# GpSimd's list scatters in a two-layer sandwich kernel: six at a step's end split in three and three, and the last eight spread in pairs over four blocks

## The chip, the cores and the metric

The kernel runs on one core of a Trainium2 chip. The metric is device time in microseconds of one execution. A core has five engines with an instruction queue each: TensorE (PE in the profile), VectorE (DVE), ScalarE (ACT), GpSimd (POOL) and SyncE (SP), which here only issues DMAs. Each executes its own queue in order; they meet through semaphores.

## The reference, cut to what matters

The input is 4096 tokens of 128 numbers (16 sequences of 256). A layer of causal linear attention with 16 heads is followed by a mixture of experts (a shared one and 8 routed ones, 2 for each token), each with a LayerNorm before and after.

```python
x = x + layernorm(attention(layernorm(x)))
xf = layernorm(x)
shared = gelu(xf @ Wfc_s + bfc_s) @ Wproj_s + bproj_s
probs = softmax(xf @ Wr)                       # 8 experts
topk_p, topk_i = top_k(probs, 2)               # gates, renormalised
routed = sum over e of (gelu(xf @ Wfc[e] + bfc[e]) @ Wproj[e] + bproj[e]) * gate[:, e]
x = x + layernorm(shared + routed)
```

## The kernel before

**Two phases.** The first goes through the tokens in NS = 8 groups of 512 (a group is 4 tiles of 128 tokens). The function `iteration(i, head, tail, nxt, routed)` of each engine is one step: in step i the head does group i's attention, the tail group i-1's output norms, and the routed part sends group i-2's tokens to their experts. Steps 0, 1, 2, 7 and 8 are written out; steps 3 to 6 are one hardware loop (`all_iterations`, L338 to L348). The second phase goes through NB = 39 blocks of 256 rows, each of one expert: `step(b, n, turn)` of each engine does block b's part of a pipeline three blocks deep.

**Lists.** Each expert has a list of rows in device memory (`expert_lists`). For each group, ScalarE copies the normed rows twice, with the number of the result row behind each (`rows_of`), VectorE works out a place in the lists for each (`route_pos`), and GpSimd writes them with eight indirect DMAs, one for each tile and choice (`scatters(i, first, last)`, L675, issued at L686). In step i the eight scatters are group i-2's.

**GpSimd's order in a step** (L741 to L791) is written by hand. In a step of the loop it is: `inv_std(1, i)` (L620 to L627, the norm of the attention's output, which waits for VectorE's `mean_var`, L1609); `route_gaps` and `route_chosen` (L694, L701); the last two scatters of the step before; `last_pairs` (L710, a fourth of the products of keys and values); Z parts 0, 1 and 2 (L767, L777, L782, factors of TensorE's output products at L1311), with the residual X (L772) and `placed` and `acc` (L733, L735) between them; `inv_std2` (L610 to L615, the norm before the experts); and then scatters 0 to 5 of this step. In step 7 scatters 0 to 4 stand there, and in step 8 the order is another.

**The logits' copy** is `a.activation(lg...)` at L1057 on ScalarE. It frees the bank in which TensorE then sums the denominators (L1414), and VectorE's `route_top` (L1705) starts from it. It increments `lg_read`, first in step 2, so that after step i's copy the semaphore stands at i-1. Ahead of it ScalarE has in a step: the rest of x (L1020), the switch of its table (L1021) and the next group's first norm (L871).

**Blocks.** In block b GpSimd's `scatter_block` waits for `blk_yr`, which VectorE raises once block b's results are in SBUF (L2124), and issues two indirect DMAs into `expert_results` (L807). At its b = 2 it first issues all eight scatters of the last group (NS - 1), whose places VectorE has ready in its own step 4. SyncE loads each block's weights (L468, 578 KB) and rows (L475, 129 KB), up to NBUF = 6 blocks ahead. Blocks 0 to 12 are made from rows of the groups scattered early; ahead of block 13 (CLOSES_AT) SyncE waits in `lists_closed` (L449 to L453) for all scatters of all groups (`scattered_late`, L452) and for the lists' tails. TensorE turns block b's rows at L1355 and multiplies at L1505 to L1507 and L1532.

Of the kernel before, what the change touches and what calls it, by code (L numbers as in the profile page):

```python
# [19 lines left out]
TILES = 4  # L20
# [21 lines left out]
def sandwich_kernel(nc, x, w_qkv, b_qkv, w_out, b_out, wfc_s, bfc_s, wproj_s, bproj_s, wr, wfc, bfc, wproj,  # L42
# [4 lines left out]
    NS = TOKENS // STEP  # L47
# [31 lines left out]
    with ExitStack() as ctx:  # L79
# [6 lines left out]
        def sem(name):  # L86
            return ctx.enter_context(nc.semaphore(name))
# [211 lines left out]
        s = {n: sem(n) for n in names}  # L299
# [9 lines left out]
        def alone(eng):  # L309

            eng.sem_inc(s["waited"], 1)
# [54 lines left out]
        def second_set(i):  # L366

            return int(isinstance(i, int) and i == NS)
# [167 lines left out]
        def _(pool):  # L536
# [36 lines left out]
            def inv_std0_early():  # L573

                a, b = TILES, 4 * TILES
                pool.wait_ge(s["ln0_mv"], 4)
                g.tensor_scalar(ve0[:, a:b], mv0[:, a:b, 1], 1.0, LN_EPS, ALU.mult, ALU.add)
                g.tensor_scalar(neg_mean0[:, a:b], mv0[:, a:b, 0], -1.0, None, ALU.mult)
                g.tensor_scalar(neg_sum0[:, 0:b], mv0[:, 0:b, 0], -float(D), None, ALU.mult
                                ).then_inc(s["ve0_ready"], 1)  # L580
                pool.wait_ge(s["ve0_ready"], 2)
                root0(a, b, 2)
# [34 lines left out]
            def inv_std(which, count):  # L617

                pool.wait_ge(s[f"ln{which}_mv"], count)
                g.tensor_tensor(ve[:, which], mv[:, which, :, 1], ln_eps[:], ALU.add)  # L620
                g.tensor_tensor(neg_mean[:, which], mv[:, which, :, 0], minus_one[:], ALU.mult
                                ).then_inc(s[f"ve{which}_ready"], 1)
                pool.wait_ge(s[f"ve{which}_ready"], count)
                g.tensor_tensor(rstd[:, which], ve[:, which], neg_half[:, 0:TILES], ALU.pow
                                ).then_inc(s[f"pow{which}_done"], 1)
                pool.wait_ge(s[f"pow{which}_done"], count)
                g.tensor_tensor(shift[:, which], neg_mean[:, which], rstd[:, which], ALU.mult  # L627
                                ).then_inc(s[f"ln{which}_rstd"], 1)
# [46 lines left out]
            def scatters(i, first, last):  # L675

                if first == 0:
                    pool.wait_ge(s["pos_ready"], i - 1)
                    pool.wait_ge(s["rows_ready"], i - 1)
                    alone(pool)  # L680
                pos, rows = pos_of_step[second_set(i)], rows_of_step[second_set(i)]
                landed = s["scattered"]
                if isinstance(i, int) and i - 2 >= COUNTED:
                    landed = s["scattered_mid" if i - 2 == COUNTED else "scattered_late"]
                for m in range(first, last):
                    g.indirect_dma_start(  # L686
                        out=lists, out_offset=bass.IndirectOffsetOnAxis(ap=pos[:, m:m + 1], axis=0),
                        in_=rows[:, m // TILES, m % TILES, :], in_offset=None).then_inc(landed, 16)

            def route_gaps(i):  # L690

                pool.wait_ge(s["top_ready"], 2 * TILES * (i - 2) + TILES)
                gaps = gap[:, bass.ds(TILES * (i - 2), TILES)]
                g.tensor_tensor(gaps, top[:, :, 1], top[:, :, 0], ALU.subtract).then_inc(s["idx_ready"], 1)  # L694

            def route_chosen(i):

                pool.wait_ge(s["hot_ready"], i - 1)
                if from_on(i, 3):
                    pool.wait_ge(s["rank_done"], i - 2)  # L700
                g.tensor_tensor(chosen[:], onehot[:, 0], onehot[:, 1], ALU.add).then_inc(s["chosen_ready"], 1)  # L701

            def last_pairs(i):

                pool.wait_ge(s["k_copied"], i + 3)
                if from_on(i, 1):
                    pool.wait_ge(s["z_ready"], 3 * i)
                for pair in range(3 if from_on(i, FREE) else 2, 4):
                    pool.wait_ge(vr_in[pair], 64 * (i + 1))
                    g.tensor_tensor(KV[:, 2 * pair:2 * pair + 2], keys.unsqueeze(1).broadcast_to([P, 2, STEP]),  # L710
                                    vr[:, 2 * pair:2 * pair + 2], ALU.mult).then_inc(s["kv_last"], 1)
# [10 lines left out]
            def rest_of_weights():  # L722

                pool.wait_ge(s["w1s_hi"], 1)
                g.tensor_tensor(w1s_lo[:], w1s_sb[:], w1s_hi[:].bitcast(F32), ALU.subtract
                                ).then_inc(s["w1s_lo"], 1)
# [10 lines left out]
            def before_next(i):  # L737

                return 5 if isinstance(i, int) and i == NS - 1 else 6

            def iteration(i, head, tail, nxt, routed):  # L741

                if isinstance(i, int) and i == 1:
                    last_pairs(1)
                if tail:
                    inv_std(1, i)
                if isinstance(i, int) and i == 0:
                    inv_std0_early()
                if isinstance(i, int) and i == 1:
                    rest_of_weights()  # L750
                if head and routed:
                    route_gaps(i)
                    route_chosen(i)
                if from_on(i, 3) and head:
                    scatters(i - 1, before_next(i - 1), 2 * TILES)
                if isinstance(i, int) and i == 0:
                    means_late()
                if head and not (isinstance(i, int) and i == 1):
                    last_pairs(i)
                if not head:  # L760
                    scatters(i - 1, before_next(i - 1), 2 * TILES)
                if head:
                    pool.wait_ge(s["kv_sum"], 4 * i + 1)
                    pool.wait_ge(s["qn_copied"], i + 1)
                    if from_on(i, 1):
                        pool.wait_ge(s["out_done"], i)
                    g.tensor_tensor(Z[:, 0], KV[:, 0], qn[:], ALU.mult).then_inc(s["z0_ready"], 1)  # L767
                if tail:
                    pool.wait_ge(s["attn_ready"], i)
                    sum_of_x1(i)  # L770
                    Xs = X[:, bass.ds(TILES * (i - 1), TILES), :]
                    g.tensor_tensor(Xs, Xs, attn[:], ALU.add).then_inc(s["x1_ready"], 1)  # L772
                if not head:
                    scatters(i, 0, 1)
                    inv_std2(i)
                if head:
                    g.tensor_tensor(Z[:, 1], KV[:, 1], qn[:], ALU.mult).then_inc(s["z1_ready"], 1)  # L777
                if head and routed:
                    route_placed(i)
                if head:  # L780
                    pool.wait_ge(s["kv_sum"], 4 * i + 2)
                    g.tensor_tensor(Z[:, 2], KV[:, 2], qn[:], ALU.mult).then_inc(s["z1_ready"], 1)  # L782
                if isinstance(i, int) and i == 0:
                    zeds_of_first()
                if tail and head:
                    inv_std2(i)
                if isinstance(i, int) and i == 1:
                    inv_std0_late()
                    fill_pads()
                if routed:  # L790
                    scatters(i, 0 if head else 1, before_next(i) if head else 2 * TILES)  # L791

            all_iterations(pool, iteration)

            def scatter_block(b, n, turn):
                if isinstance(b, int) and b == 2:
                    scatters(NS + 1, 0, 2 * TILES)
                last = isinstance(b, int) and b >= NB - HALVED
                if last:
                    pool.wait_ge(s["half_yr"], b + 1 - NB + HALVED)  # L800
                else:
                    pool.wait_ge(s["blk_yr"], b + 1)
                    alone(pool)
                for c in range(2):
                    if last and c:
                        pool.wait_ge(s["blk_yr"], b + 1)
                    g.indirect_dma_start(  # L807
                        out=results,
                        out_offset=bass.IndirectOffsetOnAxis(ap=yrow[n][:, c], axis=0),
                        in_=yb[n][:, c, :], in_offset=None).then_inc(blk_scat[n], 16)  # L810
# [1397 lines left out]
```

## Time and profile before

| | |
|---|---|
| median of 3 executions | 372.18 us |
| lowest, highest | 369.17 us, 475.82 us |
| the profiled execution: its span | 373.1 us |
| TensorE busy in it | 336.1 us (90%) |
| GpSimd busy in it | 275.8 us (74%) |
| mean granted clock of TensorE | 0.979 of full speed |

The span is from the first to the last instruction of one profiled execution, the only figure that the profile has for its own time. "Busy" is the time in which an engine had an instruction in execution; an indirect DMA counts on GpSimd for as long as GpSimd takes to write its descriptors, and the data move after that. The busy shares are averages over both phases.

### The profile page before, as it was taken

The numbers are of one execution on the slowest core, as the hardware profiler recorded it, in microseconds if no ns is written. First come the engines' busy times: TensorE is split into PE (matmuls) and PEld (weight loads), VectorE is DVE, ScalarE is ACT, GpSimd is POOL, SyncE is SP. The second block draws the span as 40 slices with busy tenths as digits, with TensorE's granted clock in tenths as the row PEclk, the third lists the DMA queues.
The fourth block names the chain that finished last, engine by engine and source line by source line (L and its number), as shares of the span: only waits on it lengthen the run. The fifth ranks groups of instructions, "written<-read, shape, count | busy, mean of one in ns | idle before, by whom it ended". The sixth has DMA issues, their size and how long they took to land.

```text
span 373.1 us, 8565 instructions
## 1 busy us (share of the span) xinstructions
PE 336.1 (90%) x2515; PEld 293.8 (79%) x2522; DVE 286.7 (77%) x716; ACT 271.3 (73%) x700; POOL 275.8 (74%) x365
## 2 busy tenths in 40 slices
PE   7767878998889889989989989979999999999993
PEld 3437457787678768877868879979999999999973
DVE  4999886999889888988995666764545539888766
ACT  4959467889868877888855878644665576689774
POOL 7878787877977869678788887777775556588760
PEclk9989999999999998989999999998999999999998
DMA  6576743967282520712605926997988769999237
GB/s 203 157 214 185 177 138 89 186 175 187 85 220 68 147 92 14 199 47 67 174 23 159 321 77 195 275 269 254 279 259 258 253 217 362 375 295 285 71 128 226
DMA packets 53515, 69.09 MB, mean 185 GB/s; under 512 B 6365, under 2 KB 37386, under 8 KB 53482
## 3 DMA queue, kind: packets, MB, share of 16 engines
q1 hardware_dynamic: 47556, 58.58, 54.7%
q0 software_dynamic: 4544, 9.35, 7.4%
q10 hardware_dynamic: 1382, 0.79, 0.8%
q8 instruction: 12, 0.20, 0.2%
q14 instruction: 21, 0.17, 0.1%
HBM read 40.06 MB, written 18.15 MB: 156 GB/s over the span
## 4 chain that ended last, share of the span: by engine, by line
PE 32%; POOL 16%; issue 11%; DVE 7%; DMA 6%; ACT 6%; SPq 2%; ACTq 1%; POOLq 1%; DVEq 0%
PE bO L1532 6%; PE bO L1311 5%; PE bS L1532 5%; DMA xb<-expert_lists 5%; POOL expert_results L807 4%; POOL expert_lists L686 2%; POOL KV L710 2%; POOL Z L777 2%; POOL X L772 2%; PE bA L1283 2%; PE bV L1506 1%; PE bV L1507 1%; PE bV L1505 1%; DMA expert_results<-yb,yrow 1%; POOL Z L767 1%
## 5 line engine op out<-in xcount | busy, mean ns | idle before, releaser
L807 POOL DMA_INDIRECT expert_results<-yb,yrow x78 | 79.2, 1015 | 36.7 <-issue 20.2
L686 POOL DMA_INDIRECT expert_lists<-rows,pos x64 | 65.0, 1016 | 22.4 <-issue 21.8
L1683 DVE TENSOR_TENSOR_SCAN KV<-bS,KV 128x1024 f32<-128x1024 bf16 x32 | 72.8, 2277 | 0.8
L1311 PE MATMUL bO<-wout_rot,Z 128*128 128x128 f32 x512 | 63.5, 278 | 7.7 <-POOL Z L777 2.3
L1311 PEld LDWEIGHTS bO<-wout_rot,Z 128*128 128x128 f32 x512 | 60.1, 192 | 12.5 <-POOL Z L777 3.2
L1137 ACT ACTIVATE hs<-bV,KV 128x256 f32<-128x256 f32 x56 | 21.9, 474 | 13.0 <-PE bV L1507 13.0
L1532 PE MATMUL bO<-KV,hs 128*128 128x128 f32 x232 | 30.1, 284 | 0.8 <-ACT hs L1137 0.8
L2116 DVE COPY yrow<-xb 128x2 int32<-128x2 int32 x24 | 4.6, 193 | 33.2 <-PE bO L1532 16.7
L1283 PE MATMUL bA<-w2s_sb,hs 128*128 128x128 f32 x224 | 30.1, 285 | 0.0
L1532 PEld LDWEIGHTS bO<-KV,hs 128*128 128x128 f32 x232 | 28.5, 199 | 1.3 <-ACT hs L1137 1.3
L1283 PEld LDWEIGHTS bA<-w2s_sb,hs 128*128 128x128 f32 x224 | 28.0, 200 | 0.1
L710 POOL TENSOR_TENSOR KV<-shared,vr 128x1024 f32<-128x1024 f32 x10 | 23.6, 2361 | 5.9 <-ACT shared L963 5.6
L1674 DVE TENSOR_TENSOR KV<-bV,vr 128x1024 f32<-128x1024 f32 x22 | 25.8, 1200 | 0.0
L1505 PE MATMUL bV<-x_lo,w_hi 128*128 128x256 f32 x80 | 24.0, 300 | 0.0
L1532 PE MATMUL bS<-Z,hs 128*128 128x128 f32 x192 | 23.3, 275 | 0.0
L1532 PEld LDWEIGHTS bS<-Z,hs 128*128 128x128 f32 x192 | 22.4, 192 | 0.0
L1506 PE MATMUL bV<-x_hi,w_hi 128*128 128x256 f32 x80 | 22.4, 280 | 0.0
L1507 PE MATMUL bV<-x_hi,w_lo 128*128 128x256 f32 x80 | 22.4, 279 | 0.0
L1691 DVE TENSOR_TENSOR Z<-KV,bV 128x1024 f32<-128x1024 f32 (+1 forms) x22 | 21.6, 1010 | 0.0
L1137 ACT ACTIVATE hs<-bA,Z 128x256 f32<-128x256 f32 x24 | 10.1, 470 | 14.9 <-PE bB L1507 14.9
L856 ACT ACTIVATE xn<-X,shift,rstd 128x128 f32<-128x128 f32 (+1 forms) x32 | 13.2, 483 | 8.6 <-POOL shift L615 8.3
L856 ACT ACTIVATE shared<-bO,shift,rstd 128x128 f32<-128x128 f32 x32 | 14.2, 462 | 4.4 <-POOL shift L627 4.4
(373 smaller groups left out, 1005.7 us busy)
## 6 DMA issues: line engine op xcount, KB each, us to landing
KV<-packed_weights SPq DMA_DIRECT2D x21, 578.0 KB, 5.1
Z<-packed_weights SPq DMA_DIRECT2D x18, 578.0 KB, 5.4
xb<-expert_lists SPq DMA_DIRECT2D x39, 129.0 KB
vr<-vr SPq DMA_DIRECT2D x16, 224.0 KB, 2.5
shared<-expert_results SPq DMA_DIRECT2D x7, 512.0 KB, 5.5
vr<-vr SPq DMA_DIRECT2D x16, 192.0 KB, 2.5
vr<-vr SPq DMA_DIRECT2D x16, 160.0 KB, 2.4
vr<-vr SPq DMA_DIRECT2D x16, 128.0 KB
```

The lines of the kernel that those rows point to most:

```text
L686: g.indirect_dma_start(out=lists, out_offset=bass.IndirectOffsetOnAxis(ap=pos[:, m:m + 1], axis=0), in_=rows[:, m // TILES, m % TILES, :], ...
L710: g.tensor_tensor(KV[:, 2 * pair:2 * pair + 2], keys.unsqueeze(1).broadcast_to([P, 2, STEP]), vr[:, 2 * pair:2 * pair + 2], ALU.mult).then ...
L807: g.indirect_dma_start(out=results, out_offset=bass.IndirectOffsetOnAxis(ap=yrow[n][:, c], axis=0), in_=yb[n][:, c, :], in_offset=None).th ...
L856: ins = a.activation(dst(j), src(j), ACT.Identity, bias=shift[:, which, j:j + 1], scale=rstd[:, which, j:j + 1], accum_out=None if total i ...
L1137: ins = a.activation(hb[m % 2][:, c], blk_h[m % 2][c // 2][:, (c % 2) * BLK:(c % 2 + 1) * BLK], ACT.Gelu_apprx_tanh, bias=wb[m][:, B1_AT + ...
L1283: ins = t.matmul(bA[:, j * D:(j + 1) * D], hs[:, c, j * P:(j + 1) * P], w2s_sb[:, c], start=False, stop=True, skip_group_check=True)
L1311: ins = t.matmul(bO[:, j * D:(j + 1) * D], Z[:, d, j * P:(j + 1) * P], wout_rot[:, d], start=False, stop=True, skip_group_check=True)
L1505: t.matmul(h, w[0], x_lo[m % 2][:], start=True, stop=False)
L1506: t.matmul(h, w[0], x_hi[m % 2][:], start=False, stop=False)
L1507: ins = t.matmul(h, w[1], x_hi[m % 2][:], start=False, stop=True)
L1532: ins = t.matmul(bank_y[:, r * D:(r + 1) * D], hb[m % 2][:, c, r * P:(r + 1) * P], wb[m][:, HID + c * D:HID + (c + 1) * D], start=(c == 0 ...
L1683: v.tensor_tensor_scan(w, ps_keep, w, 0.0, ALU.mult, ALU.add).then_inc(s["kv_sum"], 1)
```

## The change

In steps 2 to 6 GpSimd issues scatters 0, 1 and 2 at the step's end, then waits until `lg_read` is at least i, then issues scatters 3, 4 and 5. `alone` is an instruction that only increments a semaphore nobody waits for. Step 7 (five scatters at the end) and step 8 stay as they were. In the block phase `scatters(NS + 1, ...)` is called for blocks 2 to 5 with two scatters each, each pair ahead of that block's own two result scatters. Nothing else differs.

```diff
                 if isinstance(i, int) and i == 1:
                     inv_std0_late()
                     fill_pads()
-                if routed:
+                if routed and head and not (isinstance(i, int) and i == NS - 1):
+                    scatters(i, 0, 3)
+                    pool.wait_ge(s["lg_read"], i)
+                    alone(pool)
+                    scatters(i, 3, before_next(i))
+                elif routed:
                     scatters(i, 0 if head else 1, before_next(i) if head else 2 * TILES)
...
             def scatter_block(b, n, turn):
-                if isinstance(b, int) and b == 2:
-                    scatters(NS + 1, 0, 2 * TILES)
+                if 2 <= b < 2 + TILES:
+                    scatters(NS + 1, 2 * (b - 2), 2 * (b - 2) + 2)
                 last = isinstance(b, int) and b >= NB - HALVED
```

## Rows read from the trace of the kernel before

**Rows 1.** The page: the span, and each engine's busy time, share and instructions.

```profile
span 373.1 us, 8565 instructions
PE 336.1 (90%) x2515; PEld 293.8 (79%) x2522; DVE 286.7 (77%) x716; ACT 271.3 (73%) x700; POOL 275.8 (74%) x365
```

**Rows 2.** Timeline, GpSimd, one step: start, duration, line, tiles [idle before <-releaser].

```profile
127.66 0.20 POOL L615 TENSOR_TENSOR shift<-neg_mean,rstd 128x4 f32<-128x4 f32 x1
128.45 1.09 POOL L686 DMA_INDIRECT expert_lists<-rows,pos  x1 [0.58 <-issue]
129.84 1.24 POOL L686 DMA_INDIRECT expert_lists<-rows,pos  x1 [0.30 <-issue]
...
135.17 0.95 POOL L686 DMA_INDIRECT expert_lists<-rows,pos  x1 [0.30 <-issue]
137.61 0.20 POOL L620 TENSOR_TENSOR ve<-mv,ln_eps 128x4 f32<-128x4 f32 x1 [1.48 <-DVE mv L1609]
...
149.16 1.26 POOL L782 TENSOR_TENSOR Z<-KV,shared 128x512 f32<-128x512 f32 x1
151.45 0.19 POOL L610 TENSOR_SCALAR ve<-sq 128x4 f32<-128x4 f32 x1 [1.03 <-ACT shared L902]
```

**Rows 3.** Timeline, ScalarE, the logits' copy in the same step.

```profile
136.46 0.17 ACT L1057 ACTIVATE lg<-bB 128x32 f32<-128x32 f32 x1
```

**Rows 4.** Timeline, VectorE, the same step.

```profile
129.55 0.69 DVE L1936 SCALAR_TENSOR_TENSOR shared<-shared 128x512 f32<-128x512 f32 x1
...
137.16 0.36 DVE L1609 BATCH_NORM_AGGREGATE mv<-bst 128x2 f32<-128x6 f32 x4
...
149.12 0.22 DVE L1756 TENSOR_REDUCE pos<-placed 128x8 int32<-128x64 f32 x1 [0.16 <-POOL placed L733]
149.25 2.34 DVE L1691 TENSOR_TENSOR Z<-KV,bV 128x1024 f32<-128x1024 f32 x2
```

**Rows 5.** Chain of waits that ended last, the same step's end: start, length, what.

```profile
150.56 4.73 PE bO L1311 x40
...
160.49 0.86 ACT shared L871 x2
```

**Rows 6.** Timeline, ScalarE: the copy in step 3 and in step 7.

```profile
87.32 0.17 ACT L1057 ACTIVATE lg<-bB 128x32 f32<-128x32 f32 x1
184.61 0.17 ACT L1057 ACTIVATE lg<-bB 128x32 f32<-128x32 f32 x1
```

**Rows 7.** Timeline, GpSimd: the first instruction of `inv_std(1)` in step 3 and in step 7.

```profile
88.46 0.20 POOL L620 TENSOR_TENSOR ve<-mv,ln_eps 128x4 f32<-128x4 f32 x1 [0.42 <-DVE mv L1609]
186.91 0.20 POOL L620 TENSOR_TENSOR ve<-mv,ln_eps 128x4 f32<-128x4 f32 x1 [0.48 <-DVE mv L1609]
```

**Rows 8.** Timeline, GpSimd, block phase: last group's first and last scatter, then blocks'.

```profile
234.88 0.96 POOL L686 DMA_INDIRECT expert_lists<-rows,pos  x1 [0.31 <-issue]
...
244.51 0.96 POOL L686 DMA_INDIRECT expert_lists<-rows,pos  x1 [0.31 <-issue]
245.77 1.41 POOL L807 DMA_INDIRECT expert_results<-yb,yrow  x1 [0.30 <-issue]
...
254.31 0.95 POOL L807 DMA_INDIRECT expert_results<-yb,yrow  x1 [0.30 <-issue]
```

**Rows 9.** One line's instructions (L452): xcount: duration min/median/max, first and last start.

```profile
L452 SPq EVENT_SEMAPHORE  x1: 28/28/28, 252.5 to 252.5; - x1
```

**Rows 10.** Line L686 over the whole span: time from issue to landing.

```profile
DMA to landing us min/median/max: 2.3/5.2/8.1
```

**Rows 11.** Timeline, SyncE's queue: block 13's rows are issued.

```profile
255.82 0.38 SPq L475 DMA_DIRECT2D xb<-expert_lists  x1
```

**Rows 12.** Chain of waits, block phase: TensorE turns block 13's rows.

```profile
262.65 0.22 PE bH L1355 x2
```

**Rows 13.** Two steps: stretch, length, busy (x instructions) by engine, PEclk, DMA share, GB/s.

```profile
112.10:136.60 24.50, 21.59 (x154) 18.11 (x155) 21.74 (x39) 20.17 (x49) 19.73 (x26) 1.00 0.40 113
136.60:161.40 24.80, 22.98 (x154) 19.60 (x155) 21.92 (x39) 20.32 (x50) 19.17 (x26) 0.93 0.33 95
```

## The prediction, on record before the result

> **What bounds the kernel now.** I began with the page [rows 1]: TensorE is busy 90% of the 373.1 us and GpSimd 74%, but these are averages over two phases, and the first part of the change acts in the first phase alone. So I read one step of the loop, engine by engine, to see who waits for whom at the place that the change touches.
>
> GpSimd's timeline [rows 2] has six scatters from 128.45 to 136.12 (first, second and last are shown; the three between took 0.95 to 0.96 us, with 0.30 us ahead of each), then 1.48 us of idle time until VectorE's `mean_var` [rows 4] ended at 137.5, then `inv_std(1)` at 137.61. From there to 150.42, the end of Z part 2 (L782), GpSimd has no wait of any size: `inv_std(1)`, two scatters, L710, three Z parts, X, `placed`. Who needs their end? VectorE sat 0.16 us until GpSimd's `placed` before it could reduce the places, and its last two Z parts stand behind that [rows 4]. TensorE's forty output products start at 150.56, 0.14 us behind GpSimd's Z part 2, and the chain of waits goes through them and on to ScalarE's L871 ahead of the next logits' copy [rows 5]. So a step is a loop: copy, mean_var, GpSimd's run of 12.8 us, TensorE's products, the norm's transposes, ScalarE, next copy. The period is 24.5 to 24.8 us [rows 13]. What the reader is to see: the six scatters at the step's end are not on that loop. They fill time in which GpSimd would only wait for `mean_var`, and 1.48 us is left over.
>
> **First part of the change, the wait.** After step i's copy `lg_read` is i-1, so a wait for i in step i is a wait for the copy of step i+1. In the shown step it ended at 136.63 [rows 3]. Scatters 0 to 2 would be issued at about 132.3, after which GpSimd idles 4.3 us. It then has three scatters to do where it had none: the start after a release, at 0.6 us (the 0.58 us ahead of the first scatter at 128.45), then 1.05 + 0.30 + 0.96 + 0.30 + 0.96 = 3.57 us (the first of a run near 1.09, the later ones at 0.96, the gaps 0.30) [rows 2]. So `inv_std(1)` starts 4.25 us behind the copy (136.63 + 4.25 = 140.9) instead of 137.61, which is 0.98 us behind it. The step's loop is 3.27 us longer.
>
> Queued behind the waiting instruction are three scatters and then the whole run that TensorE and VectorE wait for. What could absorb it? `mean_var` needs only the copy and stays. ScalarE's norm of the attention output would start late, but is not last at Z part 0. VectorE's sum of the last pair waits for L710 and starts late with it, VectorE's 0.16 us wait for `placed` becomes 3.4 us, TensorE's wait for Z the same. The 1.03 us that GpSimd idles for ScalarE's squares [rows 2] lies behind Z part 2, beside the forty products, and I read it as slack of the second norm alone: it gives nothing back to the loop. I cost no gain from it.
>
> The wait stands at the end of steps 2 to 6, so it meets the copies of steps 3 to 7, five times. In step 3 the distance from copy to `inv_std(1)` is 88.46 - 87.49 = 0.97 us, and I take the same for steps 4 and 6. In step 7 it is 186.91 - 184.78 = 2.13 us, because the early table's work stands ahead of `mean_var` on VectorE there [rows 6, 7]. There the delay is 4.25 - 2.13 = 2.1 us. Sum: 4 x 3.27 + 2.1 = **15.2 us**.
>
> Bounds of this term: with a start of 0.15 us and the shortest scatters throughout (3 x 0.96 + 2 x 0.30 = 3.48) it is 3.63 us behind the copy, 2.65 a step, 12.1 in all. Above, if each moved scatter were stretched as the second one in [rows 2] is (1.24 against 0.96), 0.84 us more a step, 19.4 in all.
>
> That second scatter is worth a look. It ran beside VectorE's L1936 at 129.55 [rows 4], whose operands all lie in SBUF; the others ran beside instructions with an operand in PSUM. I take 0.96 us for the moved ones, since what follows the copy on VectorE (maxima, statistics, the product of keys and values from PSUM) is no such instruction. The Trainium skill, "SBUF — State Buffer", section "Who interferes with whom", says that VectorE and GpSimd share one pair of SBUF ports under an exclusive lock, taken by VectorE when it has two SBUF inputs or runs in its two-port mode. By that rule the step's end is a bad place for descriptor writing and a place behind the copy a good one, which speaks for the change; what it would give back is the 0.28 us of one scatter, which stays where it is. With it or without it the sum is 15.2.
>
> The moved scatters' data land 8 us later than now. `rows_of` and `route_pos` of the next step wait for all eight of a group, of which the last two are issued behind `inv_std(1)` as before, so these set that wait and move with the step. No cost of its own.
>
> **Second part, the pairs.** GpSimd now issues the last group's eight scatters from 234.88 to 245.47 and then the results of block 2 and on, running late on all of them [rows 8]. With pairs, the results of blocks 2, 3 and 4 (six scatters) come ahead of the eighth. Six took from 245.77 to 254.31, 8.5 us, so the eighth starts at 253.0 instead of 244.5 on the clock of now. The number of instructions is the same and GpSimd is back in step with VectorE at the same time; the results of blocks 2 to 4 land sooner, for which nobody was waiting.
>
> Who waits for the eighth is SyncE, ahead of block 13: its wait for it passed at 252.5, 8.0 us after the issue [rows 9]. Landing takes 2.3 to 8.1 us, median 5.2 [rows 10]. The new wait ends at 255.3 to 261.1, at 258.2 with the median: 5.7 us later (2.8 to 8.6). Block 13's rows were issued at 255.82 [rows 11] and turned by TensorE at 262.65 [rows 12], 6.8 us of room. Issued 5.7 us later, at 261.5, they land between 2.3 us on (the shortest landing of a smaller transfer) and 6.8 us on (they were there in that time now). I take 3.7 us, nearer the short end, since the queues run empty while SyncE waits: 265.2, and TensorE stalls **2.5 us**. The early end with the short landing gives no stall, the late one with 6.8 us gives 8.6. The loads of block 14 and on come late too, but TensorE is then late as well, so it costs once.
>
> **Sum.** 373.1 + 15.2 + 2.5 = 390.8 on the profiled span. That span lies 0.9 above the median of the runs, and the lowest run 3.0 below the median; the same sum on the median gives 389.9. I say 389.
>
> **Rivals.**
>
> TensorE's clock adds to it. In the second of the two steps [rows 13] the granted clock was 0.93 in the mean: (1 - 0.93) x 24.8 / 0.5 = 3.5 us of it at the lower level, 1.2 of 2.4 GHz. That step was 0.3 us longer. With 3.3 us more of idle time in each step there may be more such stretches. If each of five took 1.7 us of the forty products (3.5 us at half speed), that is 8.5 more: 398. Against it: a step with the same idle time ran at 1.00.
>
> Part of the delay is absorbed. If VectorE's and TensorE's paths beside GpSimd's have less need of it than I read (for instance GpSimd's two later scatters overlap with a wait that I can't see), the step grows by 1.5 instead of 3.3 and the block phase by nothing: 372.2 + 7.5 = 380. For it: the 1.03 us of idle time ahead of `inv_std2`. Against it: 0.16 and 0.14 us are all the slack the rows show.
>
> Not slower: the copy is done before GpSimd asks for it. Its place is the wait at the end of the step, its price zero, and it decides where the copy comes before 132.3, the end of scatter 2; then the three scatters follow without a gap and all stays at 372. It needs the release to be 4.3 us earlier than the copy in [rows 3], or the semaphore to run one step ahead of my count. A gain over 2% would need scatters that hold up VectorE or ScalarE now; the rule on the shared port is what could give that, and VectorE's idle times there are for the copy and not for GpSimd.
>
> **How the numbers follow.** 0.74 for the forecast (384 to 394), 0.12 for the clock (394 to 399), 0.08 for the part absorbed (378 to 384), 0.06 for no delay. A change of 2%, 7.4 us, is about what a measurement of this kernel can tell from none: below 379.6 is "same". The last case is nearly all same, with 0.01 of it for a gain, and the absorbed case gives 0.01 to it as well. The range takes the forecast with the lower end of the first term (372.2 + 12.1 = 384, and 2 less for a low median) up to most of the clock's case: 382 to 398.
>
> **What would show it.** Right: GpSimd idle 4 us ahead of the fourth scatter with ScalarE's copy as its end; no more idle time ahead of L620; the copies in steps 4 to 6 some 27.8 us apart instead of 24.6; VectorE 3 us idle ahead of L1756; SyncE's L452 passed some 5.7 us later on the block phase's own clock, and TensorE idle for block 13's rows. Wrong: copies still 24.6 us apart (the delay was hidden), or more than 28.5 apart with a clock well under 0.9 (the clock took its share), or a block phase of unchanged length (the second part is free).

## The result and the profile after

The changed kernel took 392.1 us in the median of 4 runs (389.21 to 394.11), the kernel before 373.0 us in the median of 4. The ratio is 1.0541, with a 95% interval of 1.0493 to 1.0589: 20 us slower. Runs more than 1.5% above the fastest of the same kernel, such as the one of 475.82 us of the kernel before, stand in the medians of this document and not in its ratios. The profiled execution has a span of 387.5 us against 373.1, only 14.4 more, because the two profiled executions are not typical ones: that of after was the fastest of its four runs (389.21 us, 1.7 above its span), while that of before, whose span alone is 373.1, lies above its kernel's median.

```profile
span 387.5 us, 8570 instructions
PE 341.8 (88%) x2515; PEld 295.4 (76%) x2522; DVE 285.5 (74%) x716; ACT 272.0 (70%) x700; POOL 275.0 (71%) x365
```

Beside [rows 1], VectorE, ScalarE and GpSimd are busy for the same time to within 1.2 us, in a longer span; GpSimd's is even 0.8 less. What was added is waiting, and 5.7 us of TensorE, which is busy longer with the same number of instructions. The timeline of GpSimd over a step's end, after (start, duration, line, tiles, idle time before and its releaser), is the counterpart of [rows 2]:

```profile
134.67 1.09 POOL L686 DMA_INDIRECT expert_lists<-rows,pos  x1 [0.58 <-issue]
136.06 1.25 POOL L686 DMA_INDIRECT expert_lists<-rows,pos  x1 [0.30 <-issue]
137.62 0.96 POOL L686 DMA_INDIRECT expert_lists<-rows,pos  x1 [0.30 <-issue]
144.36 0.96 POOL L686 DMA_INDIRECT expert_lists<-rows,pos  x1 [5.78 <-ACT lg L1062]
145.62 0.96 POOL L686 DMA_INDIRECT expert_lists<-rows,pos  x1 [0.30 <-issue]
146.88 0.96 POOL L686 DMA_INDIRECT expert_lists<-rows,pos  x1 [0.30 <-issue]
147.86 0.22 POOL L620 TENSOR_TENSOR ve<-mv,ln_eps 128x4 f32<-128x4 f32 x1
```

(Lines behind 790 stand 5 further on in the changed kernel: the copy is L1062 there, `mean_var` L1614.) The copy ended at 143.54. The fourth scatter starts 0.82 us behind it, and L620, the head of the run that everybody waits for, 4.32 us behind it. In [rows 2, 3] that distance was 0.98. The 1.48 us for which GpSimd waited for `mean_var` are gone from the row of L620.

Now the whole time, stretch by stretch. The cuts are the logits' copy of steps 3 to 7, TensorE's turning of block 0, of block 9 and of block 14, and the end. Each row of this view has: from and to, length, busy time of PE, PEld, DVE, ACT and POOL with instruction counts, TensorE's granted clock, DMA share, GB/s. First the kernel before:

```profile
87.32:111.92 24.60, 21.60 (x154) 18.11 (x155) 21.73 (x39) 20.21 (x50) 20.46 (x27) 1.00 0.58 151
111.92:136.46 24.54, 21.59 (x154) 18.11 (x155) 21.74 (x39) 20.21 (x49) 19.73 (x26) 1.00 0.40 114
136.46:161.26 24.80, 22.98 (x154) 19.60 (x155) 21.92 (x39) 20.32 (x49) 19.03 (x26) 0.93 0.33 95
161.26:184.61 23.35, 22.47 (x157) 19.41 (x159) 20.84 (x35) 18.86 (x46) 18.34 (x26) 0.93 0.34 98
184.61:210.02 25.41, 23.27 (x168) 19.25 (x167) 18.97 (x74) 15.66 (x42) 21.62 (x31) 1.00 0.42 137
210.02:244.77 34.75, 32.72 (x301) 31.80 (x300) 23.82 (x87) 26.97 (x69) 27.36 (x30) 1.00 0.72 202
244.77:265.90 21.13, 19.07 (x152) 18.74 (x151) 10.37 (x31) 10.21 (x26) 16.30 (x16) 0.92 0.92 263
265.90:373.10 107.20, 100.50 (x854) 97.89 (x852) 72.41 (x243) 74.54 (x193) 64.73 (x67) 0.99 0.77 250
```

The same eight stretches of the kernel after:

```profile
85.02:114.80 29.78, 24.69 (x154) 20.81 (x155) 21.83 (x39) 20.46 (x49) 19.74 (x26) 0.89 0.51 135
114.80:143.37 28.57, 24.37 (x154) 20.53 (x155) 21.94 (x39) 20.54 (x49) 19.73 (x26) 0.88 0.28 83
143.37:171.24 27.87, 22.48 (x154) 18.32 (x155) 21.83 (x39) 20.48 (x49) 19.71 (x26) 1.00 0.29 85
171.24:197.73 26.49, 21.96 (x157) 18.41 (x159) 21.41 (x38) 18.99 (x46) 19.72 (x26) 1.00 0.30 89
197.73:226.44 28.71, 24.86 (x168) 19.82 (x167) 18.65 (x72) 15.46 (x42) 23.64 (x33) 0.94 0.39 118
226.44:260.17 33.73, 32.51 (x302) 31.75 (x301) 22.77 (x87) 26.86 (x69) 26.05 (x29) 1.00 0.72 214
260.17:280.80 20.63, 17.72 (x152) 17.15 (x151) 10.53 (x31) 10.31 (x26) 16.05 (x16) 1.00 0.85 246
280.80:387.50 106.70, 100.60 (x854) 97.83 (x852) 72.40 (x243) 74.44 (x193) 64.31 (x68) 0.99 0.80 255
```

The differences are +5.18, +4.03, +3.07, +3.14, +3.30, then -1.02, -0.50 and -0.50. They make +16.7, and the copy of step 3 came 2.3 us earlier, a difference that stands already at step 2's copy, where the two kernels are alike: +14.4. So the loss lies in the five steps, as +18.7 us, and the block phase of this execution lost nothing against this execution of before.

The cleanest pair is 27.87 against 24.54, both at a clock of 1.00: **+3.33 us a step.** The first two steps lost more, at a granted clock of 0.89 and 0.88. TensorE's forty products show it, in its timeline after:

```profile
98.13 1.16 PE L1316 MATMUL bO<-wout_rot,Z 128*128 128x128 f32 x8 [1.81 <-POOL Z L767]
100.72 2.08 PE L1316 MATMUL bO<-wout_rot,Z 128*128 128x128 f32 x8 [1.43 <-POOL Z L777]
103.01 6.07 PE L1316 MATMUL bO<-wout_rot,Z 128*128 128x128 f32 x40 [0.22 <-issue]
```

They took 6.07 us here and 4.73 in [rows 5]. TensorE had sat idle 1.8 and 1.4 us for GpSimd's Z just ahead; then the eight products and the first half of the forty ran at the lower level (the granted clock of 100 to 106 is 0.50). The same idle times stand in steps 5 and 6, which ran at 1.00, so the idle time does not decide it. Over steps 3 to 6 of the profiles taken where the kernel before takes 371 to 373 us, 13 of 16 steps were below 1.00 in the four profiles of kernels with scatters behind the copy (9 of 12 without the long run of four and two), and 6 of 20 in the five profiles of kernels with none. More idle time and more such steps go together here; that one makes the other is not shown. The kernel before is one of the latter: its two steps at 0.93 had the lower level just behind the logits' copy (0.50 from 163 to 166 in the second), after TensorE had sat idle for 1.2 us.

VectorE, after, waited for GpSimd in two places instead of the one of [rows 4]:

```profile
155.19 2.29 DVE L1688 TENSOR_TENSOR_SCAN KV<-bS,KV 128x1024 f32<-128x1024 bf16 x1 [3.14 <-POOL KV L710]
...
159.36 0.22 DVE L1761 TENSOR_REDUCE pos<-placed 128x8 int32<-128x64 f32 x1 [1.30 <-POOL placed L733]
```

In the block phase, TensorE's turning of blocks 10, 12 and 13 after:

```profile
264.06 0.44 PE L1360 MATMUL bT<-ident,xb 128*128 128x128 f32 x2 [0.37 <-DMA xb<-expert_lists]
...
271.58 0.38 PE L1360 MATMUL bT<-ident,xb 128*128 128x128 f32 x2
277.33 0.44 PE L1360 MATMUL bH<-ident,xb 128*128 128x128 f32 x2 [2.16 <-DMA xb<-expert_lists]
```

Block 13 stalled for its rows, 5.75 us behind block 12 where 3.42 is the undisturbed distance. SyncE's side of it, after: its wait for the scatters, and the issue of block 13's rows, beside [rows 9, 11].

```profile
L452 SPq EVENT_SEMAPHORE  x1: 28/28/28, 271.4 to 271.4; - x1
```

```profile
273.41 0.38 SPq L475 DMA_DIRECT2D xb<-expert_lists  x1
```

But before had a stall of its own, at block 10, in its TensorE timeline:

```profile
244.77 0.38 PE L1355 MATMUL bH<-ident,xb 128*128 128x128 f32 x2
...
250.41 0.44 PE L1355 MATMUL bT<-ident,xb 128*128 128x128 f32 x2 [2.06 <-DMA xb<-expert_lists]
...
255.65 0.38 PE L1355 MATMUL bH<-ident,xb 128*128 128x128 f32 x2
```

From block 9 to block 14 it took 21.13 us where five undisturbed blocks take 17.1: 4.0 lost, with a stretch of low clock behind the stall (block 10 to 11 took 5.24). That is why the table shows no loss there. The four other kernels that issue the last eight in a row (the split alone, four and two, seven and eight at the end, below) stalled for 0.5 to 1.5 us at block 10 and took 18.5 to 19.5 us for that stretch, so this profile of before is the long one of its kind.

### The profile page after: what moved, and what is told of

The parts are those of the page before. It is cut to its first block, busy times and chain, and to the rows that moved or that the text cites. A ratio compares the mean times of both kernels' runs of the same rounds, so it can differ in the third digit from the quotient of the medians.

```text
span 387.5 us, 8570 instructions
## 1 busy us (share of the span) xinstructions
PE 341.8 (88%) x2515; PEld 295.4 (76%) x2522; DVE 285.5 (74%) x716; ACT 272.0 (70%) x700; POOL 275.0 (71%) x365
## 4 chain that ended last, share of the span: by engine, by line
PE 37%; POOL 19%; issue 12%; ACT 8%; DMA 3%; DVE 3%; POOLq 1%; ACTq 1%; SPq 0%; DVEq 0%
PE bO L1316 9%; PE bO L1537 6%; PE bS L1537 6%; POOL expert_lists L686 4%; POOL expert_results L812 4%; POOL KV L710 3%; ACT shared L861 2%; POOL Z L767 2%; PE bV L1511 2%; POOL Z L777 2%; PE bV L1510 2%; PE bV L1512 2%; POOL X L772 2%; ACT shared L876 1%; DMA xb<-expert_lists 1%
## 5 line engine op out<-in xcount | busy, mean ns | idle before, releaser
L812 POOL DMA_INDIRECT expert_results<-yb,yrow x78 | 78.0, 1000 | 36.1 <-issue 19.3
L686 POOL DMA_INDIRECT expert_lists<-rows,pos x64 | 65.8, 1028 | 46.1 <-ACT lg L1062 25.6
L1316 PE MATMUL bO<-wout_rot,Z 128*128 128x128 f32 x512 | 67.8, 289 | 20.6 <-POOL Z L767 10.3
L1316 PEld LDWEIGHTS bO<-wout_rot,Z 128*128 128x128 f32 x512 | 63.8, 202 | 27.7 <-POOL Z L767 14.3
L1537 PE MATMUL bO<-KV,hs 128*128 128x128 f32 x232 | 28.9, 277 | 0.8 <-ACT hs L1142 0.8
L1288 PE MATMUL bA<-w2s_sb,hs 128*128 128x128 f32 x224 | 29.0, 278 | 0.0
L1537 PEld LDWEIGHTS bO<-KV,hs 128*128 128x128 f32 x232 | 27.2, 192 | 1.3 <-ACT hs L1142 1.3
L1288 PEld LDWEIGHTS bA<-w2s_sb,hs 128*128 128x128 f32 x224 | 26.8, 193 | 0.1
L710 POOL TENSOR_TENSOR KV<-shared,vr 128x1024 f32<-128x1024 f32 x10 | 23.5, 2355 | 4.3 <-ACT shared L968 3.8
L1202 PE MATMUL bH<-zeros 128*128 128x512 bf16 x56 | 17.6, 471 | 1.6 <-POOL bias_raw L539 1.3
```

Source lines behind the costliest of these rows:

```text
L686: g.indirect_dma_start(out=lists, out_offset=bass.IndirectOffsetOnAxis(ap=pos[:, m:m + 1], axis=0), in_=rows[:, m // TILES, m % TILES, :], ...
L812: g.indirect_dma_start(out=results, out_offset=bass.IndirectOffsetOnAxis(ap=yrow[n][:, c], axis=0), in_=yb[n][:, c, :], in_offset=None).th ...
L1288: ins = t.matmul(bA[:, j * D:(j + 1) * D], hs[:, c, j * P:(j + 1) * P], w2s_sb[:, c], start=False, stop=True, skip_group_check=True)
L1316: ins = t.matmul(bO[:, j * D:(j + 1) * D], Z[:, d, j * P:(j + 1) * P], wout_rot[:, d], start=False, stop=True, skip_group_check=True)
L1537: ins = t.matmul(bank_y[:, r * D:(r + 1) * D], hb[m % 2][:, c, r * P:(r + 1) * P], wb[m][:, HID + c * D:HID + (c + 1) * D], start=(c == 0 ...
```

## Experiments

**Theories.** Mine: in each of five steps the scatters behind the copy delay the head of GpSimd's run, the loop grows by what they take, and the pairs add a stall at block 13. Rivals: the wait itself (a release, an instruction more) is what costs; TensorE's clock is the larger part; the pairs carry the loss.

The first runs of the split alone, the pairs alone, the wait behind six and four and two met a chip on which the kernel before takes 413 us, and the second run of the wait behind six one on which it takes 420. All others met a chip on which it takes 371 to 372. Only the latter carry sizes.

### The split alone (two runs)

```diff
-                if routed:
+                if routed and head and not (isinstance(i, int) and i == NS - 1):
+                    scatters(i, 0, 3)
+                    pool.wait_ge(s["lg_read"], i)
+                    alone(pool)
+                    scatters(i, 3, before_next(i))
+                elif routed:
```

> The wait and the three scatters behind it in steps 2 to 6, with the last group's eight scatters as before. Theory (the three scatters stand on GpSimd's run, which the step's loop goes through; the pairs cost 2.5 us at block 13 on their own): steps some 3.3 us longer where the clock stays up, the first phase 15 to 19 us longer, ratio 1.042 to 1.052; no stall ahead of block 13's rows. Rival (the pairs give back about what they cost, as the block phase of the changed kernel, no longer than before, suggests): the same ratio as the whole change, 1.054 within 0.004.

Measured: 418.68 us, ratio 1.0234 (1.0138 to 1.0330), against 413.42.

> The split alone again, now that the kernel before takes 372 us in other calls. Theory: nearly the whole cost, ratio 1.042 to 1.055, copies of steps 3 to 6 27.7 to 29.8 us apart. If the pairs carry 2.5 us on their own, this is 0.007 under the whole change; if they give back what they cost, it is the same within 0.004.

Measured: 391.19 us, ratio 1.0539 (1.0481 to 1.0597), against 371.2. The split alone is the whole loss as far as these two ratios can tell: 0.007 for the pairs would be within their intervals. Its timeline shows the same picture as after (L620 at 118.41, its step's copy ended at 114.07: 4.34 us behind). On the slower chip the steps of an unsplit kernel are longer already. There the profile of the pairs alone, whose steps are those of the kernel before, shows the copy late (ScalarE idles 0.8 to 1.7 us ahead of it with no releaser in the core's own record) and more idle time ahead of L620 than the 1.48 us of [rows 2]:

```profile
142.00 0.20 POOL L620 TENSOR_TENSOR ve<-mv,ln_eps 128x4 f32<-128x4 f32 x1 [2.66 <-DVE mv L1609]
```

Its copies are 26.7 to 27.1 us apart in steps 3 to 6, those of the split kernel there 28.0 to 29.6. So the same edit costs some 2 us a step there.

### The pairs alone (two runs)

```diff
-                if isinstance(b, int) and b == 2:
-                    scatters(NS + 1, 0, 2 * TILES)
+                if 2 <= b < 2 + TILES:
+                    scatters(NS + 1, 2 * (b - 2), 2 * (b - 2) + 2)
```

> The last group's eight scatters in pairs over blocks 2 to 5, the steps' ends as before. Theory (they cost a stall for block 13's rows and give nothing): 2.5 us, ratio 1.004 to 1.010, SyncE passes L452 some 5 to 8 us later, TensorE idle 2 us ahead of block 13's rows. Rival (they also ease the load of block 10's rows, for which TensorE stalled 2.06 us before): that stall goes and the sum is near zero, ratio 0.997 to 1.003.

Measured: 414.45 us, ratio 1.0081 (1.0023 to 1.0138). This profile has no stall at block 13 (3.42 us behind block 12), so on the slower chip the cause of these 0.8% stays open.

> The pairs alone again. Theory of the prediction (a stall of 2.5 us for block 13's rows, nothing back): ratio 1.004 to 1.010. Rival (block 10's rows, for which TensorE stalled 2.06 us before, come sooner, since half of the descriptors ahead of them go elsewhere or the phase differs): 0.997 to 1.003, with a stall at block 13 and none at block 10. Last time it was 1.008 on a chip on which the kernel before took 413 us.

Measured: 375.72 us, ratio 1.0123 (1.0075 to 1.0171): 4.6 us of 371.2 (2.8 to 6.3). The pairs do cost, and more than I had said. The rival was right that block 10 does not stall here, and wrong that this makes up for block 13. The turning of blocks 12, 13 and 14 in TensorE's timeline of this kernel:

```profile
254.81 0.38 PE L1355 MATMUL bT<-ident,xb 128*128 128x128 f32 x2
261.56 0.69 PE L1355 MATMUL bH<-ident,xb 128*128 128x128 f32 x2 [3.02 <-DMA xb<-expert_lists]
266.35 0.38 PE L1355 MATMUL bT<-ident,xb 128*128 128x128 f32 x2
```

The stall is 3.02 us, block 13 comes 6.75 us behind block 12 and block 14 another 4.79 behind it, both beyond 3.42, at a lowered clock: 4.7 us in all. The wait for the scatters ended here at

```profile
L452 SPq EVENT_SEMAPHORE  x1: 28/28/28, 255.4 to 255.4; - x1
```

that is 45.7 us behind block 0 (turned at 209.66), where it is 42.5 before.

### The last eight as four and four

```diff
-                if isinstance(b, int) and b == 2:
-                    scatters(NS + 1, 0, 2 * TILES)
+                if 2 <= b < 4:
+                    scatters(NS + 1, 4 * (b - 2), 4 * (b - 2) + 4)
```

> The last group's eight scatters as four and four, ahead of the results of blocks 2 and 3; the steps' ends as before. Only block 2's two results come ahead of the eighth, so it goes 2.5 us later instead of 8.5. Theory (block 13's rows are late by what the eighth is late, less the slack, which was near none for 5.7 us): SyncE passes L452 about 2 to 3 us later than before, no stall or one under 0.5 us at block 13, ratio 0.996 to 1.003. Rival (any order but eight first costs the pairs' amount): 1.004 or more.

Measured: 372.6 us, ratio 1.0025 (0.9983 to 1.0068). With two results between the scatters instead of six, no loss can be told: the eighth scatter starts at 245.23, not at 252.14 as with pairs, SyncE passes at 251.5 (43.7 us behind block 0, 1.2 later than before, where I had expected 2 to 3), and TensorE's stretch from block 9 to block 14 lost 1.0 us. The windows' row of that stretch, first of the kernel with the pairs alone:

```profile
244.36:266.35 21.99, 18.97 (x152) 18.46 (x151) 10.45 (x31) 10.32 (x26) 16.81 (x18) 0.92 0.83 248
```

And of the kernel with fours:

```profile
242.50:260.57 18.07, 17.70 (x153) 17.14 (x151) 10.37 (x31) 10.30 (x26) 13.79 (x15) 1.00 0.91 268
```

The two differ by 3.9 us, the two medians by 3.1.

### The wait kept, all six scatters ahead of it (two runs)

```diff
-                if routed:
+                if routed and head and not (isinstance(i, int) and i == NS - 1):
+                    scatters(i, 0, 6)
+                    pool.wait_ge(s["lg_read"], i)
+                    alone(pool)
+                    scatters(i, 6, before_next(i))
+                elif routed:
```

(`before_next(i)` is 6 there, so nothing is behind the wait.)

> All six scatters at the step's end, and the wait for the logits' copy behind them with nothing moved behind it. Theory (the cost is the three scatters behind the wait, not the wait): GpSimd waits there for the copy and then for mean_var as before, L620 some 1 us behind the copy, ratio 0.997 to 1.004. Rival (the wait itself, its release and the instruction behind it, costs): 0.5 us or more a step, 2.5 us or more, ratio over 1.007.

Measured: 412.44 us, ratio 1.0030 (0.9979 to 1.0080).

> The whole six scatters of a step ahead of the wait for the logits' copy, nothing behind it, on a chip on which the kernel before takes about 372 us. Theory: the harm of the split is the scatters that are left behind the copy (1.26 us each and 0.8 us of release), not the wait. With none behind it, the wait ends before GpSimd's next line 620 could start anyway (0.98 us behind the copy in the kernel before, 0.8 us of it being release), so the ratio is 0.995 to 1.008 and line 620 starts within 0.5 us of where it does before. Rival: the wait in itself holds GpSimd (a slow release in each of five steps, at 0.8 us each): ratio 1.01 or more, line 620 at 1.8 us behind the copy.

Measured: 416.39 us, ratio 0.9999 (0.9949 to 1.0049). Both runs met slower chips, where L620 has more slack, so the claim holds for these. There the wait costs nothing. Its timeline, GpSimd, last scatter and L620; the copy of that step ended at 120.11:

```profile
117.10 0.96 POOL L686 DMA_INDIRECT expert_lists<-rows,pos  x1 [0.30 <-issue]
121.08 0.20 POOL L620 TENSOR_TENSOR ve<-mv,ln_eps 128x4 f32<-128x4 f32 x1 [3.02 <-DVE mv L1614]
```

L620 starts 0.97 us behind the copy, as in the kernel before in [rows 2, 3] (0.98), although GpSimd waited for the copy first: `mean_var` and its release end later than that wait. The rival that the wait itself holds GpSimd would have put it later. Of the 0.98 us nothing is the release of such a wait, as the expectation had it: L620 starts 0.09 us behind the end of `mean_var` in [rows 2, 4].

### Four ahead of the copy and two behind (two runs)

The edit is that of the split alone with 4 for 3 in both calls.

```diff
+                    scatters(i, 0, 4)
+                    pool.wait_ge(s["lg_read"], i)
+                    alone(pool)
+                    scatters(i, 4, before_next(i))
```

> Four scatters ahead of the wait and two behind it, the eight as before. Theory (each scatter behind the wait lengthens the step by its 1.26 us): L620 3.0 us behind the copy instead of 4.25, steps 2.0 us longer, 8 to 11 us in all, ratio 1.022 to 1.031. Rival (what counts is that GpSimd is held until the copy at all): the same as three and three, ratio 1.042 or more.

Measured: 418.46 us, ratio 1.0207 (1.0085 to 1.0330).

> Four ahead of the wait, two behind it. Theory (1.26 us a step for each scatter behind the wait): L620 3.0 us behind the copy, 4 x 2.0 + 0.9 = 8.9 us, ratio 1.020 to 1.030. Rival (holding GpSimd until the copy is what costs): 1.042 or more.

Measured: 386.11 us, ratio 1.0306 (1.0237 to 1.0375), between none behind and three behind. The ratio rests on the runs of 381.28 and 383.94 us alone, and the profile is of one of the two longer ones (388.27). GpSimd's timeline; the copy of this step ended at 145.62:

```profile
146.43 0.96 POOL L686 DMA_INDIRECT expert_lists<-rows,pos  x1 [4.59 <-ACT lg L1062]
147.69 0.96 POOL L686 DMA_INDIRECT expert_lists<-rows,pos  x1 [0.30 <-issue]
148.68 0.21 POOL L620 TENSOR_TENSOR ve<-mv,ln_eps 128x4 f32<-128x4 f32 x1
```

L620 is 3.06 us behind the copy: 1.26 less than with three behind, one scatter and its gap. The copies are 27.4 us apart, 0.8 more than 24.54 and the delay of 2.08 make. TensorE's timeline of this kernel has the clock in it:

```profile
132.47 2.07 PE L1316 MATMUL bO<-wout_rot,Z 128*128 128x128 f32 x8 [1.43 <-POOL Z L777]
134.76 4.97 PE L1316 MATMUL bO<-wout_rot,Z 128*128 128x128 f32 x40 [0.22 <-issue]
```

The eight took 2.07 us, against 1.16 at the full clock, in each of steps 3 to 6 of this longer run; how often the shorter ones have it is not shown.

### The whole change again

```diff
+                    scatters(i, 0, 3)
+                    pool.wait_ge(s["lg_read"], i)
...
+                if 2 <= b < 2 + TILES:
+                    scatters(NS + 1, 2 * (b - 2), 2 * (b - 2) + 2)
```

> The whole change once more, beside one part and beside another length of GpSimd's work. On the chip of the four experiments before this one the kernel before itself took 413 us and its steps 26.7 us, with TensorE's results arriving later than its records end; the split alone cost 1.023 there. Theory (the cost is GpSimd's run becoming 3.3 us longer, and where something else already lengthens the steps a part of it is absorbed): about 1.05 where the kernel before takes 372 us, 1.02 to 1.035 where it takes 413 us. Rival (the pairs carry a good part of the cost): over 1.05 on either.

Measured: 392.71 us, ratio 1.0574 (1.0485 to 1.0664), against 372.1. Its copies of steps 3 to 7 are 27.92, 29.74, 28.57 and 26.46 apart, at granted clocks of 0.94, 0.89, 0.88 and 1.00: about 27.9 and 26.5 again, and two longer steps at a lowered clock, one of them another than in the first profile. The result is what both the theory and the rival had for this chip, so it does not say what share the pairs have.

### The other way: seven, then all eight, at the step's end

If scatters on the loop are the harm, the two that stand between `route_chosen` and `last_pairs` in the kernel before do harm too. These kernels move one or both to the step's end, with no wait.

```diff
-                return 5 if isinstance(i, int) and i == NS - 1 else 6
+                return 5 if isinstance(i, int) and i == NS - 1 else 7
```

> Seven scatters at the end of steps 2 to 6 and one in the next step behind inv_std(1), no wait, the eight as before. The other direction: it takes one scatter (1.26 us) off the run between inv_std(1) and L710 and puts it into the 1.48 us in which GpSimd waited for mean_var. Theory: GpSimd's run is 1.26 us shorter, VectorE and TensorE, which have 0.1 to 1.2 us of slack beside it, become the bound: 1 to 4 us faster, ratio 0.989 to 0.998. Rival (the run is not what sets the step): 0.998 to 1.003.

Measured: 368.69 us, ratio 0.9896 (0.9821 to 0.9970). GpSimd's timeline:

```profile
135.81 0.22 POOL L620 TENSOR_TENSOR ve<-mv,ln_eps 128x4 f32<-128x4 f32 x1
...
146.23 1.26 POOL L782 TENSOR_TENSOR Z<-KV,shared 128x512 f32<-128x512 f32 x1
```

L620 is 1.01 us behind the copy's end (134.80), so in this step the seventh scatter just filled what was idle (in steps 3, 4 and 6 L620 came 1.44 to 1.85 us behind it), and the run from L620 to the end of L782 is 11.68 us, 1.13 less than the 12.81 of [rows 2]. The next copy came 23.44 us behind this one, 1.10 less than 24.54.

```diff
-                return 5 if isinstance(i, int) and i == NS - 1 else 6
+                return 5 if isinstance(i, int) and i == NS - 1 else 8
```

> All eight scatters at the end of steps 2 to 6. Theory: L620 starts 1.0 us later (the eighth reaches past mean_var), the two behind inv_std(1) are gone, 2.7 us less, so GpSimd's run ends 1.7 us earlier and others bind: the same ratio as seven at the end within 0.003, 0.988 to 0.999. Rival (any scatter beyond mean_var costs the step its full 1.26 us): 1.003 to 1.012.

Measured: 368.42 us, ratio 0.9842 (0.9768 to 0.9917): **this beats both kernels.** GpSimd's timeline:

```profile
140.72 0.22 POOL L620 TENSOR_TENSOR ve<-mv,ln_eps 128x4 f32<-128x4 f32 x1
...
142.92 2.36 POOL L710 TENSOR_TENSOR KV<-shared,vr 128x1024 f32<-128x1024 f32 x1
...
149.55 1.28 POOL L782 TENSOR_TENSOR Z<-KV,shared 128x512 f32<-128x512 f32 x1
```

Here L620 is late (2.81 us behind the copy, 1.83 more than before), but its run up to L782's end at 150.83 is 10.11 us, 2.70 less; the difference, 0.87 gained, is what the step shows (23.66 against 24.54). Seven and eight can't be told apart by their intervals.

## Why the prediction was right, and which of its sizes were not

**The delay of a step (3.27 us predicted).** Right. 4.25 us behind the copy was the estimate; 4.32 was measured, 4.34 with the split alone. The step grew by 3.33 at equal clock. The start behind the release was 0.82 us instead of the 0.6 that I took, and the first scatter of the new run 0.96 instead of the 1.05 in the sum; and 0.6 and 3.57 make 4.17, not the 4.25 that I wrote. So part of the close agreement is luck: added up rightly, the terms give 3.19 us a step and 14.8 in all. Two behind instead of three takes 1.26 us off; none behind takes all of it off, on the slower chips. In step 7 the distance became 4.31 us where it was 2.13: 2.2 for the 2.1 predicted (the stretch there grew by 3.30, with a clock of 0.94 for 1.00 in it). The term of 15.2 is 15.5 by these (4 x 3.33 + 2.2).

**The shared port.** The second scatter of the step's end took 1.25 us again and the three behind the copy 0.96 each. The Trainium skill's rule ("SBUF — State Buffer", section "Who interferes with whom") has a condition that the prediction left out: a VectorE instruction with two SBUF inputs contends with a GpSimd instruction that reads SBUF, not with one that only writes it. No run here shows whether that is what stretched the second scatter. The place behind the copy does cost less for each scatter, but 0.28 us of one descriptor's writing is nothing beside three scatters that nobody covers any more.

**Nothing absorbs it.** Right in sum, with a detail off. I had VectorE 3.4 us idle ahead of the reduction of the places (now L1761). It sat 3.14 us ahead of the last pair's sum, for L710, and 1.30 ahead of L1761. The first of the two was in the prediction as "starts late with it" but not counted as where the idle time would show.

**The stall at block 13 (2.5 us).** The size came out, 2.16 of idle time and 2.3 of distance, but by luck: its errors cancel. I took the median landing, 5.2 us; the eighth scatter, issued at 267.96, had landed at 271.4, 3.4 us later, perhaps since with pairs it goes out when the queues have little of such work (no run isolates that). So SyncE passed 2.5 us later on the block phase's clock, counted from block 0 (45.0 against 42.5), not 5.7. It then issued block 13's rows 2.0 us behind that instead of the 3.3 of [rows 9, 11], so they went out only 1.2 us later than before (47.0 against 45.8). They were turned 3.9 us behind their issue, near the 3.7 that I took. And the room of 6.8 us that I read from [rows 11, 12] contained 4.0 us by which TensorE was late from block 10. In the kernel with fours, without that stall, block 13 is turned 49.2 us behind block 0 and not 52.5, which leaves a room of 3.4 us instead of 6.8. Less delay met less room. The step that was mis-sized is "they were there in that time now": I measured slack in a stretch that held a stall of another cause, one row of the windows away at a granted clock of 0.92. Alone, the pairs cost 1.0123, 4.6 us, for 2.5.

**The sum.** 389 said, 392.1 measured, inside 382 to 398. From step 3's copy to block 0 the kernel before took 122.7 us, the two profiles of the whole change 141.4 and 140.6, that of the split alone 142.8: 17.9 to 20.1 us more, of which 15.5 is the term above. The other 2.4 to 4.6 I put to TensorE's lower level, which more of the steps had than before. So the clock's rival came true in part, as some 2 to 5 us and not 8.5, and a sign that I had named for it came up: copies 29.8 and 28.6 us apart at 0.89 and 0.88. What a stretch at that level costs differs: in the first profile step 3 lost 1.85 us beyond the 3.33 and step 4 lost 0.70, in the second step 3, at 0.94, lost nothing. The four runs of the changed kernel go the same way: 389.21, 391.85, 392.34 and 394.11 us at clocks of 0.972, 0.964, 0.963 and 0.959.

From block 0 to the end the profile of before took 163.1 us. The four other kernels that issue the last eight in a row took 159.1 to 160.6 there, 160.1 in the mean, and the three profiles with pairs 161.1, 163.2 and 163.3, 162.5 in the mean. An estimate of the pairs' cost from these means is 2.4 us. With the 17.9 and 18.7 us ahead of block 0 that makes 20 to 21 us for the whole change, against 20 measured. "A block phase of unchanged length", my sign that the second part is free, came up in the first pair of profiles and misled, since the one of before is longer than others of its kind.

**The rivals.** The absorbed part (380) fell: no row has a step that grew by less than 3.07. Not slower fell too: the wait was for the copy of the next step, as 3.7 to 7.0 us of idle time ahead of the fourth scatter show. Its gain of over 2% has no trace of support.

**Open.** The ratios of the parts do not add well. On top of the split, which alone is 1.0539, the pairs' 1.2% should give 1.067, with an interval of its own of about 1.059 to 1.074, and the whole is 1.0541 and 1.0574. The first (up to 1.0589) stays below that; the second (up to 1.0664) does not contradict it. The profiles have 20.63 us from block 9 to block 14 with the whole change and 18.78 with the split alone, so 1.9 us of the pairs' cost there. The second profile of the whole change has 21.32, with a low stretch of the clock that the first lacks:

```profile
261.09:282.41 21.32, 19.11 (x152) 18.73 (x151) 10.38 (x31) 10.82 (x26) 16.44 (x17) 0.92 0.86 256
```

So the cost at block 13 differs from execution to execution, and one or two profiles of each kernel don't fix its mean. Nor was the wait behind six tried on the faster chip.

## What to carry to other kernels

Work that fills an engine's wait is free only there. Before moving it past a semaphore, find what the engine does next and who waits for that; each instruction moved behind the release is added to the loop in full where, as here, nothing else holds the loop up. The same reading, turned round, finds the gain: look for work with a late deadline that stands inside the loop's run and move it into the wait, even a little beyond its end, as long as more comes off the run than is added ahead of it. And when slack is read from two rows, look for another stall between them first.

## What the runs showed of the hardware

- The first indirect DMA behind the wait for ScalarE's copy started 0.81 to 0.82 us behind the copy's end, in every step read. That is not what every GpSimd instruction takes: L620 starts 0.09 us behind the end of VectorE's `mean_var` in [rows 2, 4]. An indirect DMA behind another started 0.30 us behind it and took mostly 0.96 us of GpSimd, 1.09 as the first of a run and 1.24 to 1.25 as the second at a step's end.
- The time from the last scatter's issue until SyncE's wait for it passed differed between the kernels: 8.0 us in the kernel before, 7.9 with the split alone, 6.3 with fours, 2.8 to 3.4 for the last of the pairs; on the slower chip it was 8.7 for the last of the pairs.
- TensorE's lower clock level, 1.2 GHz or 0.50 of full speed, came for some 3.4 to 6.9 us (from the granted clocks of the windows) in some steps and not in others with the same idle times. With scatters behind the copy, where TensorE sat idle 1.0 to 1.8 us twice ahead of its output products, it came in 13 of 16 steps; without them in 6 of 20.
- The same program took 371 to 372 us on one chip and 413 and 420 on two others. On the slower ones ScalarE waited up to 8.0 us, in the blocks, for something that the core's own record doesn't name (no profile from the faster chip has such a wait), and TensorE's mean clock was 0.93 against 0.98. Ratios got there are not the ratios of the faster chip: the split is 1.023 on one and 1.054 on the other.
